# A graph network's edge stages make the receivers' projection themselves

## What is computed

```python
h = x @ W_enc.T + b_enc
for l in range(2):
    m = relu(concat([h[src], h[dst]]) @ msg_W1[l].T + msg_b1[l])
    m = m @ msg_W2[l].T + msg_b2[l]
    agg = segment_sum(m, dst)
    upd = concat([h, agg]) @ upd_W[l].T + upd_b[l]
    h = layer_norm(h + upd)
out = h @ W_out.T + b_out
```

## Time and profile before

| | us |
|---|---|
| median of 3 runs | 3886.1 (3885.23 to 3891.72) |
| profiled execution, its own time | 3925.8 |
| span of the profiled execution | 3924.1 |
| PE busy | 3146.7 (80%) |
| VectorE busy | 2686.3 (68%) |
| ScalarE busy | 2361.9 (60%) |
| GpSimd busy | 1817.9 (46%) |

### The profile page before, as it was taken

How to read it: one execution, slowest core, us unless ns; L and a number is a source line. 1 busy time by engine, 2 the same in 40 slices (tenths; PEclk the granted TensorE clock), 3 DMA queues, 4 the chain that set the end, 5 groups by cost and what they waited for, 6 DMA issues and landing times. The chain is left out here.

```text
span 3924.1 us, 93325 instructions
## 1 busy us (share of the span) xinstructions
PE 3146.7 (80%) x25312; PEld 2796.9 (71%) x25312; DVE 2686.3 (68%) x8634; ACT 2361.9 (60%) x5642; POOL 1817.9 (46%) x1782
## 2 busy tenths in 40 slices
PE   4966537766556789978999876999969998778998
PEld 3743326554443379978998776999969988768998
DVE  9999747765436688865666544666647665547998
ACT  3789707655432268875665543566646665436999
POOL 0000133556664533334555564655444555665664
PEclk9989968988778999999999997999989999989999
DMA  0046516765438989995665432899956654426987
GB/s 18 2 143 225 165 38 185 196 173 157 131 100 279 337 294 366 358 331 167 192 187 169 138 110 62 297 323 330 315 190 193 191 173 148 122 72 215 295 295 248
DMA packets 460716, 777.83 MB, mean 198 GB/s; under 512 B 113688, under 2 KB 115864, under 8 KB 460392
## 3 DMA queue, kind: packets, MB, share of 16 engines
q1 hardware_dynamic: 355046, 548.85, 42.3%
q10 hardware_dynamic: 67714, 147.73, 11.0%
q0 software_dynamic: 37632, 77.15, 7.8%
HBM read 451.50 MB, written 321.78 MB: 197 GB/s over the span
## 5 line engine op out<-in xcount | busy, mean ns | idle before, releaser
L885 DVE SCALAR_TENSOR_TENSOR edges_acc<-edges_acc,keep,edges_ps_a 128x128 f32 (+1 forms) x2352 | 820.2, 349 | 374.2 <-remote 121.3
L853 POOL DMA_INDIRECT ring<-table_p,esrc x784 | 760.1, 970 | 640.8 <-PE edges_ps_m L1014 329.8
L1013 PE MATMUL edges_ps_m<-ring,ident 128*128 x3136 | 646.6, 288 | 125.5 <-POOLq L843 50.7
L1014 PE MATMUL edges_ps_m<-edges_q_ring,edges_turned 128*128 x3136 | 632.5, 284 | 27.0 <-issue 26.7
L870 DVE TENSOR_TENSOR edges_onehot<-iota,drel 128x512 f32<-128x512 f16 x441 | 303.6, 689 | 443.5 <-DMA table_p<-nodes_p_out 299.4
L1013 PEld LDWEIGHTS edges_ps_m<-ring,ident 128*128 128x128 f32 x3136 | 499.1, 200 | 148.4 <-issue 98.0
L981 ACT ACTIVATE edges_msg<-edges_ps_m 128x512 f32<-128x512 f32 x392 | 231.4, 590 | 614.3 <-PE edges_ps_m L1014 241.9
L1014 PEld LDWEIGHTS edges_ps_m<-edges_q_ring,edges_turned 128*128 128x128 f32 x3136 | 499.4, 200 | 36.0 <-issue 35.6
L1023 PE MATMUL edges_ps_a<-edges_onehot,edges_msg 128*128 128x128 f32 x3136 | 437.4, 284 | 69.6 <-issue 63.1
L853 POOL DMA_INDIRECT ring<-table_h,esrc x344 | 328.2, 954 | 308.3 <-PE edges_ps_a L1038 157.1
L1023 PEld LDWEIGHTS edges_ps_a<-edges_onehot,edges_msg 128*128 128x128 f32 x3136 | 397.9, 199 | 82.8 <-issue 81.6
(11 more groups left out here) (315 smaller groups left out, 6869.5 us busy)
## 6 DMA issues: line engine op xcount, KB each, us to landing
table_z<-nodes_z_t SPq DMA_DIRECT2D x196, 256.0 KB, 5.0
table_p<-nodes_p_out SPq DMA_DIRECT2D x196, 256.0 KB
table_q<-nodes_q_out ACTq DMA_DIRECT2D x196, 256.0 KB
edges_q_ring<-table_q SPq DMA_DIRECT2D x196, 256.0 KB
edges_d_ring<-table_d ACTq DMA_DIRECT2D x98, 512.0 KB
table_t<-edges_acc SPq DMA_DIRECT2D x196, 256.0 KB
nodes_in_a<-table_t SPq DMA_DIRECT2D x196, 256.0 KB
nodes_in_z<-table_z SPq DMA_DIRECT2D x196, 256.0 KB, 4.5
```

The lines of the kernel that those rows point to most:

```text
L853: nc.gpsimd.indirect_dma_start(out=ring[:, e % RE * W:e % RE * W + P], out_offset=None, in_=table[:, :], in_offset=bass.IndirectOffsetOnAx ...
L885: nc.vector.scalar_tensor_tensor(out=to, in0=to, scalar=m.keep[:, s:s + 1], in1=ps_a[:, i % AR, where(j):where(j) + F], op0=ALU.mult, op1= ...
L1013: nc.tensor.matmul(to, m.ident[:], rows[j], start=True, stop=False)
L1014: last = nc.tensor.matmul(to, turned[:, i % QR, j * P:(j + 1) * P], slots[j], start=False, stop=True)
```

## The change

nodes-1 and nodes0 no longer multiply, copy or store q. A layer's edge stage makes it: it loads a chunk of the turned rows z from `table_z` to `z_in` (a ring of 4), PE multiplies it by q's weights to one of two PSUM banks (`product_q`), and VectorE copies it out. Chunks 0 to 7 go straight into `q_ring`; later ones go to `q_out` (a ring of 5), from which ScalarE stores them to `table_q`, and SP loads them back to `q_ring` as before, after a wait for that store (`kept_q`). Products 0 to 7 come ahead of batch 0, product i+8 in batch i between `segment` and `combine`, so the last is in batch 89 of 196. SP issues the first 10 loads of z, ScalarE the others, and ScalarE the stores of q.

```diff
+ZR, QO, LEAD = 4, 5, 8
...
+        def load_z(eng, c):
+            if c >= ZR:
+                eng.wait_ge(s_made_q, c - ZR + 1)
+            eng.dma_start(z_in[:, c % ZR, :], m.table_z[layer][turn_back(c) * P:(turn_back(c) + 1) * P, :]).then_inc(s_z[c % ZR], 16)
+
+        def kept_q(eng, c):
+            eng.wait_ge(s_kept_q[(c - RC) % QO], 16 * ((c - RC) // QO + 1))
+
+        def copy_q(eng, copy, c):
+            eng.wait_ge(s_made_q, c + 1)
+            if c >= RC + QO:
+                kept_q(eng, c - QO)
+            to = q_ring[:, c * CH:(c + 1) * CH] if c < RC else q_out[:, (c - RC) % QO, :]
+            copy(to, ps_q[:, c % 2, :]).then_inc(s_copied_q, 1)
...
 SyncE
-                    for c in range(RC):
-                        sp.dma_start(q_ring[:, c * CH:(c + 1) * CH], chunk(table_q, turn_back(c))).then_inc(s_q[0] if c else s_q_first, 16)
-                    sp.wait_ge(s_q_first, 16)
+                    for c in range(LEAD + 2):
+                        load_z(sp, c)
+                    sp.wait_ge(s_copied_q, 1)
                     sp.sem_inc(s_n, 1)
-                    sp.wait_ge(s_q[0], 16 * (RC - 1))
+                    sp.wait_ge(s_copied_q, RC)
...
                         if c + RC < NCHUNK:
+                            kept_q(sp, c + RC)
                             sp.dma_start(q_ring[:, at * CH:(at + 1) * CH], chunk(table_q, turn_back(c + RC))).then_inc(s_q[c % 2], 16)
...
 VectorE
+                if not degrees:
+                    for c in range(LEAD):
+                        copy_q(dve, nc.vector.tensor_copy, c)
...
                     if lag <= i < NB + lag:
                         chain(i - lag)
+                    if not degrees and i + LEAD < NCHUNK:
+                        copy_q(dve, nc.vector.tensor_copy, i + LEAD)
...
 ScalarE
                         if i + 2 < NB:
                             turn(i + 2)
+                        if i + LEAD + 2 < NCHUNK:
+                            load_z(act, i + LEAD + 2)
+                        if RC <= i + LEAD - 2 < NCHUNK:
+                            act.wait_ge(s_copied_q, i + LEAD - 1)
+                            act.dma_start(chunk(table_q, turn_back(i + LEAD - 2)), q_out[:, (i + LEAD - 2 - RC) % QO, :]).then_inc(s_kept_q[(i + LEAD - 2 - RC) % QO], 16)
                         act.wait_ge(s_pq, i + 1)
...
 TensorE
+                def product_q(c):
+                    pe.wait_ge(s_z[c % ZR], 16 * (c // ZR + 1))
+                    if c >= 2:
+                        pe.wait_ge(s_copied_q, c - 1)
+                    for j in range(J):
+                        last = nc.tensor.matmul(ps_q[:, c % 2, j * P:(j + 1) * P], z_in[:, c % ZR, j * P:(j + 1) * P],
+                                                m.wproj[:, layer, D:2 * D], start=True, stop=True)
+                    last.then_inc(s_made_q, 1)
...
                     if i >= BEHIND:
                         segment(i - BEHIND)
+                    if i + LEAD < NCHUNK:
+                        product_q(i + LEAD)
                     if i < NB:
                         combine(i)
...
+                if not degrees:
+                    for c in range(LEAD):
+                        product_q(c)
...
 node_stage
-                def evacuate_q(c, b, turn):
-                    act.wait_ge(s_proj, c + 1)
-                    if reused(c, RING):
-                        act.wait_ge(s_store["q"][b], turn * 16)
-                    nc.scalar.copy(q_out[:, b, :], ps_q[:, b % 2, :]).then_inc(s_out_q, 1)
-
-                def store_q(c, b, turn):
-                    act.wait_ge(s_out_q, c + 1)
-                    act.dma_start(chunk(m.table_q[nxt], c), q_out[:, b, :]).then_inc(s_store["q"][b], 16)
...
-                    pipelined(act, [(root_y, 2), (copy_z, 4), (norm_y, 3), (evacuate_q, 5), (store_q, 6)])
+                    pipelined(act, [(root_y, 2), (copy_z, 4), (norm_y, 3)])
...
-                        pe.wait_ge(s_v if final else s_out_q, c - 1)
-                        if not final:
-                            pe.wait_ge(s_out_p, c - 1)
+                        pe.wait_ge(s_v if final else s_out_p, c - 1)
...
-                            nc.tensor.matmul(part(ps_q, b % 2, j), part(z_t, b, j), m.wproj[:, nxt, D:2 * D], start=True, stop=True)
                             last = nc.tensor.matmul(part(ps_p, b % 2, j), part(z_t, b, j), m.wproj[:, nxt, 0:D], start=True, stop=True)
```

More of the change, by code:

```diff
@@ L764, in _, with edge_stage @@
                 act.wait_ge(s_d, 16)
-def edge_stage(nc, m, table, table_q, agg, degrees, x=None):
+def edge_stage(nc, m, table, table_q, agg, degrees, x=None, layer=None):
     F = P + 1 if degrees else P
@@ L784, in edge_stage @@
             d_ring = sb("d_ring", [P, DR, DB * CH], F16)
-            ps_m = pb("ps_m", 512, QR)
+            ps_m, ps_q = pb("ps_m", 512, QR), pb("ps_q", 512, 2)
+            z_in, q_out = sb("z_in", [P, ZR, CH]), sb("q_out", [P, QO, CH])
+            s_z, s_kept_q = [sem(f"s_z{r}") for r in range(ZR)], [sem(f"s_kept_q{r}") for r in range(QO)]
+            s_made_q, s_copied_q = sem("s_made_q"), sem("s_copied_q")
         else:
@@ L795, in edge_stage @@
         s_d = [sem(f"s_d{r}") for r in range(DR)]
-        s_out, s_q, s_go, s_q_first = [sem("s_out0"), sem("s_out1")], [sem("s_q0"), sem("s_q1")], sem("s_go"), sem("s_q_first")
+        s_out, s_q, s_go = [sem("s_out0"), sem("s_out1")], [sem("s_q0"), sem("s_q1")], sem("s_go")
         load = lambda eng, at: nc.values_load_multi_w_load_instructions(
@@ L815, in landed @@
                     if not degrees and c + RC < NCHUNK:
-                        sp.wait_ge(s_q[c % 2], 16 * (c // 2 + 1) + (16 * (RC - 1) if c % 2 == 0 else 0))
+                        sp.wait_ge(s_q[c % 2], 16 * (c // 2 + 1))
                     sp.sem_inc(s_n, 1)
@@ L1230, in node_stage @@
         else:
-            p_out, q_out, ps_p = sb("p_out"), sb("q_out"), pbank("ps_p", 2)
+            p_out, ps_p = sb("p_out"), pbank("ps_p", 2)
         s_a, s_x, s_z = sems("s_a"), sems("s_x"), sems("s_z")
-        s_store = {k: sems(f"s_store_{k}") for k in "pqzr"}
+        s_store = {k: sems(f"s_store_{k}") for k in "pzr"}
         (s_pad, s_coef, s_bias, s_sum, s_y, s_stat, s_aggr, s_std, s_rstd, s_shift, s_norm, s_flip_z, s_z_t, s_proj,
-         s_out_p, s_out_q, s_extra_m, s_extra, s_added, s_flip_x, s_v, s_stat2, s_aggr2, s_std2, s_rstd2, s_res, s_go) = (sem(n) for n in (
+         s_out_p, s_extra_m, s_extra, s_added, s_flip_x, s_v, s_stat2, s_aggr2, s_std2, s_rstd2, s_res, s_go) = (sem(n) for n in (
              "s_pad", "s_coef", "s_bias", "s_sum", "s_y", "s_stat", "s_aggr", "s_std", "s_rstd", "s_shift", "s_norm", "s_flip_z",
-             "s_z_t", "s_proj", "s_out_p", "s_out_q", "s_extra_m", "s_extra", "s_added", "s_flip_x", "s_v", "s_stat2", "s_aggr2",
+             "s_z_t", "s_proj", "s_out_p", "s_extra_m", "s_extra", "s_added", "s_flip_x", "s_v", "s_stat2", "s_aggr2",
              "s_std2", "s_rstd2", "s_res", "s_go"))
@@ L1353, in _ @@
                 else:
-                    pipelined(act, [(root_y, 2), (copy_z, 4), (norm_y, 3), (evacuate_q, 5), (store_q, 6)])
-                    for b in range(RING):
-                        act.wait_ge(s_store["q"][b], 16 * slot_uses(RING, b))
+                    pipelined(act, [(root_y, 2), (copy_z, 4), (norm_y, 3)])
             @block.tensor
@@ L1538, in build @@
         for l in range(L):
-            stage(f"edges{l}", edge_stage, m.table_p[l], m.table_q[l], m.table_t, False)
+            stage(f"edges{l}", edge_stage, m.table_p[l], m.table_q[l], m.table_t, False, None, l)
             stage(f"nodes{l}", node_stage, a["x"], out, l)
```

## The result

The changed kernel takes 4006.1 us (median of 4 runs, 4000.28 to 4006.54) against 3888.0 for the kernel before in the same comparison: ratio 1.030, 95% interval 1.0282 to 1.0318. It is 3% slower. The forecast was slower, 3959, range 3905 to 4035; the point was 47 us low.

The account below looks back on a forecast made before the run. PE was taken to bound nodes0 and the edge stages' first part, but not nodes-1 by itself. Two edge stages at 81 + 6 us, less 82 (nodes0) and 19 (nodes-1), gave +73 on the median: 3959 us, range 3905 to 4035.

Parts of the forecast that it names:

- Direction and place: Whole kernel: slower, chance 0.89; PE bounds the edge stages' first part and pays there for the products.
- Each edge batch, 2.90 to 3.80: Edge stages' first part: 8 more PE records add 0.90 us a batch, waits kept; +81 us a stage over 90 batches.
- rival D: Edge stages' first part: the product fills PE's waits, 3.59 us a batch, total +29, 3915 us; chance 0.14.
- Rival B: Edge stages' first part: z comes late, 3.95 or 4.20 us a batch, the latter +145 in total, 4031 us; chance 0.20.
- 0.56 us for VectorE's copy: Edge batches: the added copy out of PSUM takes 0.56 us, bringing VectorE from 2.05 to 2.61 us a batch.
- The start, +6: Start of each edge stage: eight products before batch 0 use up instructions PE had in hand; +6 us (0 to 15).
- nodes0, -82: nodes0: 4.04 us a chunk falls to 3.20, 0.06 over PE's bound, -82 us; 3.40 if transfers hold it (-63).
- nodes-1, -19: nodes-1: 3.45 us a chunk falls to 3.25, the spacing of two y's on VectorE, -19 us; ends -45 and -10.
- The sum: Whole kernel: 2 x (81 + 6) - 82 - 19 = +73 us, made on the profiled execution and added to the median.
- Instructions that come late: Edge stage start: the trace agrees with the skill on the loop jump, not on "mostly hidden", which would make the total 10 us less.

Follow-up runs that it names:

- a_layer1: Against the kernel before, only layer 1 makes its q in its edge stage, with nodes-1 and edges0 as before: 3960.2 us, ratio 1.009.
- a_early: The changed kernel with a z_in ring of 8 and each load of z asked for 5 batches ahead instead of 2: 3963.9 us, ratio 1.0189.
- a_noz: The changed kernel without loads of z or waits for them, the full product computed on constants: 3967.1 us, one execution.
- the third set: A group of follow-up kernels run on one chip beside the kernel before, whose median there was 3891.5 us.
- a_lags: The changed kernel with nodes0's transpose, projection, copies and store one chunk later and the update ahead of the transpose: 4000.9 us, ratio 1.0193.
- a_cheap: The changed kernel with the product's 4 float32 matmuls replaced by 4 float16 ones on constants: 4017.8 us, a single execution.

## Why the prediction was right, and where it was short

**Direction and place.** Right. PE set the pace of the edge stages' first part, the products took its time there, and the node stages gave back less. a_layer1 shows the parts in separate stages.

**Each edge batch, 2.90 to 3.80.** Measured 3.76, but made up differently. The forecast kept PE's 0.20 us of waits a batch and put 0.90 on top. Once z is in time the batch is 3.57 (a_early, and a_noz with no z at all): the product fills the old waits, as rival D had it with 3.59, and costs 0.67. Rival B's wait then brought 0.19, from its mechanism, beside the 0.15 and 0.40 that B added for a landing in 6 and in 6.5 us: loads asked about 6.5 us ahead were at times late. The term was right by luck, two errors that cancel. Two stages got 164 us longer, forecast 174. Against the 692.5 us that the same edges0 took in the third set it would be 85 and 92, and that spread between chips is as large as the term's error. The forecast's 0.56 us for VectorE's copy was misread: the earlier trace rows is a mean over two shapes, three copies of 128x512 at 0.68 and one of 128x32 at 0.18. The copies took 0.69; with 2.05 + 0.69 = 2.74 us a batch they stayed beside PE all the same.

**The start, +6.** Measured by the start of batch 3: 47.2 us after the stage's start against 37.4, less three times the batch's own difference of 0.86 us, so about +7. The size was right and the reason half right: the products did not run out of instructions first, VectorE's copies stood still.

**nodes0, -82.** This step failed: measured -56.5. "I take 3.20 us, 0.06 over PE's bound" had the engines' busy time and the DMA share checked, and not the ring of waits through ScalarE, PE and VectorE that two chunks share; it stood at 3.42 us. The forecast's low end of gain, 3.40, had the size but gave it to transfers, and a_lags shows that these were not the limit.

**nodes-1, -19.** Measured -11.4, 3.33 us a chunk instead of 3.25. This saving is known roughly: the unchanged stage took 352.5 to 359.0 us in six traces, the changed one 340.3 to 343.3 in eight. In 1450 to 1650 us of after PE's transposes stand 54.5 us in wait of z; the same ring may hold this stage, but I didn't lengthen its lags, so that is argued and not shown.

**The sum.** The two node terms were 33 us too large as gains and the edge terms 10 too large as costs: 73 + 33 - 10 = 96, the stages' sum. The other 22 us to the 118 of the medians are no step's: the forecast added a difference to the median, which is right, but its rows come from an execution of before that was 38 us longer than its median, about half of it in stages that the change doesn't touch. So the result fell inside the range for other reasons than the range was drawn for: its upper part was rival B's, and most of the shortfall came from the node stages and from the trace of before.

**Instructions that come late.** "Issue" in the rest of the stage is unchanged (53.5 against 54). The Trainium skill (Runtime: NRT & Kernel Launch, Instruction fetch mechanics) calls the crossing of a block of instructions mostly hidden. No run here shows what a crossing costs, and the forecast went too far where it had the trace agree on the jump out of a loop and disagree on this: at the start of an edge stage VectorE stands 4.29 and 11.21 us and PE 9.86 behind it, but the first transfer of instructions comes only after such a stall. That the instructions are what is late is thus argued, from the absence of any other releaser; that the stall ends with GpSimd's run of gathers is shown for two lengths of the run.

**Open.** What PE, or VectorE, lacks while GpSimd issues its run of gathers; why PE stands a second time, at the combine, after a late product; and why "issue" grows late in the stage with the shorter run of gathers.

## What to carry to other kernels

Before work is moved between stages, price it at each stage's own limit: eight records cost 0.67 us where PE set the pace, part of them in waits that it had before, and gave back 0.62 and 0.12 us a chunk where other things came next. When an engine is relieved, look for the ring of waits through several engines that will hold next; its length over the number of steps that it serves is the new pace, and no busy share shows it (PE and DMA both stood at 0.94). A load moved into a busy stage should be asked for several steps ahead, since being late cost about 17 us a stage and its traffic next to nothing.

## What the runs showed of the hardware

- A run of indirect gathers issued without a pause on GpSimd (24 in 29.7 us, 1.25 us apart) goes with stalls of other engines at the start of a stage, 4.29 and 11.21 us on VectorE; with 16 in a run PE did 261 records in the first 50 us instead of 149.
- A copy of 128x512 float32 from PSUM on VectorE took 0.69 us.
- PE's late product was followed by a second wait at the combine, of 0.65 us in after and 1.2 to 1.6 us in a_cheap, for which the trace names nothing.
- With PE full in nodes0, DMA reached a share of 0.99 at 336 GB/s; the 0.94 seen before was demand and not the limit.
- The same code ran 0.9% apart in two sets (medians 3923.6 and 3890.4 us), so a stage is better compared within a set.
